# An attention block's scores in runs of three pairs, the row maxima turned in the scores' banks, and a changed start

## The reference

```python
def attn(x, Wq, bq, Wk, bk, Wv, bv, Wo, bo):      # x: (4, 512, 256), 16 heads of 16
    Q, K, V = (...)                                # x @ W.T + b, split into heads
    scores = jnp.einsum('bhqd,bhkd->bhqk', Q, K) / jnp.sqrt(jnp.float32(Hd))
    attn = jax.nn.softmax(scores, axis=-1)
    out = jnp.einsum('bhqk,bhkd->bhqd', attn, V)
    return out.transpose(0, 2, 1, 3).reshape(B, S, D) @ Wo.T + bo
x = x + attn(layernorm(x), ...)
x = x + ffn(layernorm(x), W1, W2, W3)              # silu(x W1') * (x W3'), Hadamard transform, W2
x = x + memory(layernorm(x), ...)
x = x + ffn(layernorm(x), W1, W2, W3)
```

## Time and profile before

| what | value |
|---|---|
| median of three runs | 586.15 us |
| the profiled execution | 586.26 us, of which the span from first to last instruction is 584.4 |
| TensorE busy | 565.8 us, 97% |
| VectorE busy | 376.8 us, 64% |
| ScalarE busy | 298.5 us, 51% |
| GpSimd busy | 176.6 us, 30% |
| granted TensorE clock | 0.999 |
| DMA | 26.54 MB, mean 45 GB/s |
| chain that ended last | TensorE 85%, VectorE 5%, ScalarE 4% |

### The profile page before, as it was taken

One profiled execution on the slowest core, in us unless ns is written; L12 is line 12 of the kernel. 1 busy time (PEld: TensorE's weight loads), 2 busy tenths in 40 slices (PEclk: granted clock), 3 DMA queues, 4 the chain that ended last, 5 costly groups with the idle time before them and its releaser, 6 DMA issues.

```text
span 584.4 us, 8867 instructions
## 1 busy us (share of the span) xinstructions
PE 565.8 (97%) x3288; PEld 390.1 (67%) x3288; DVE 376.8 (64%) x718; ACT 298.5 (51%) x546; POOL 176.6 (30%) x193
## 2 busy tenths in 40 slices
PE   9899999999999988999999999999999999999997
PEld 4534334344334433368888888898777888888886
DVE  5498898898888899644363444558887436344433
ACT  3238878876886787752334242244445233424221
POOL 3956446354455242820101010014333010101000
PEclk9999999999999999999999999999999999999999
DMA  7654740240033030010000000000000010010101
GB/s 231 135 112 163 199 122 18 76 127 20 2 111 109 3 146 3 3 72 2 1 0 1 1 0 1 2 2 0 1 0 2 1 36 1 1 36 2 38 0 37
DMA packets 17891, 26.54 MB, mean 45 GB/s; under 512 B 2552, under 2 KB 10744, under 8 KB 17464
## 3 DMA queue, kind: packets, MB, share of 16 engines
q1 hardware_dynamic: 15992, 24.13, 13.6%
q10 hardware_dynamic: 1856, 1.84, 1.4%
HBM read 10.88 MB, written 5.24 MB: 28 GB/s over the span
## 4 chain that ended last, share of the span: by engine, by line
PE 85%; DVE 5%; ACT 4%; issue 2%; DMA 1%; POOL 1%; SPq 1%; DVEq 0%; ACTq 0%
PE PS L281 82%; PE PS L292 2%; DVE mxr L861 2%; ACT PR L735 1%; DMA ring<-ql 1%; DVE PR L1020 1%; ACT xf L644 1%; ACT qf L658 1%; DVE XNs L842 1%; ACT PR L788 1%; POOL xTl L1051 1%; ACT xTh L644 1%; PE PS L472 1%; DVE AOl L853 1%; SPq L214 1%
## 5 line engine op out<-in xcount | busy, mean ns | idle before, releaser
L281 PE MATMUL PS<-xTh,ring 128*128 128x512 f32 x608 | 188.5, 392 | 0.0
L861 DVE TENSOR_REDUCE mxr<-PS 128x1 f32<-128x512 f32 x256 | 163.0, 682 | 29.0 <-PE PS L281 28.7
L735 ACT ACTIVATE PR<-PS 128x512 f32<-128x512 f32 x256 | 137.8, 603 | 39.7 <-PE PS L281 39.7
L281 PEld LDWEIGHTS PS<-xTh,ring 128*128 128x128 f32 x608 | 113.2, 188 | 22.9 <-issue 0.8
L281 PE MATMUL PS<-xTl,ring 128*128 128x512 f32 x304 | 110.3, 391 | 0.4 <-POOL xTl L1051 0.4
L281 PE MATMUL PS<-ring 50*128 50x512 f32 (+1 forms) x512 | 98.2, 450 | 5.4 <-DVE mxr L861 4.9
L975 DVE TENSOR_TENSOR PR<-PR,PS 128x512 f32<-128x512 f32 x64 | 43.8, 684 | 91.6 <-PE PS L281 73.7
L281 PEld LDWEIGHTS PS<-ring 50*128 50x128 f32 (+1 forms) x512 | 41.2, 184 | 84.2 <-ACT PR L735 57.2
L644 ACT ACTIVATE AOh<-PR 128x512 fp32r<-128x512 f32 x72 | 45.5, 632 | 101.1 <-DVE PR L975 89.2
L1051 POOL TENSOR_TENSOR xTl<-xf,xTh 128x512 fp32r<-128x512 f32 x30 | 43.2, 1456 | 140.9 <-ACT xTh L644 140.9
L853 DVE TENSOR_TENSOR AOl<-PR,AOh 128x512 fp32r<-128x512 f32 x72 | 51.1, 710 | 50.3 <-ACT AOh L644 50.3
(11 more groups left out here) (98 smaller groups left out, 621.5 us busy)
## 6 DMA issues: line engine op xcount, KB each, us to landing
ring<-qh SPq DMA_DIRECT2D x52, 128.0 KB, 3.1
ring<-ql SPq DMA_DIRECT2D x26, 128.0 KB, 3.1
ring<-weight_scratch SPq DMA_DIRECT2D x3, 1024.0 KB, 4.9
weight_scratch<-in_w SPq DMA_DIRECT2D x2, 1024.0 KB, 6.8
out<-X SPq DMA_DIRECT2D x8, 256.0 KB, 2.2
X<-in_x SPq DMA_DIRECT2D x3, 512.0 KB, 5.2
PR<-in_w SPq DMA_DIRECT2D x1, 1024.0 KB, 7.6
ring<-AOh SPq DMA_DIRECT2D x8, 128.0 KB, 4.0
```

The lines of the kernel that those rows point to most:

```text
L281: return nc.tensor.matmul(dst, lhsT, rhs, start=start, stop=stop, skip_group_check=True)
L735: nc.scalar.activation(PR[:, j % 8, :], PS[:, kq_bank(j), :], ACT.Exp, scale=HD ** -0.5)\
L861: nc.vector.tensor_reduce(mxr[:, S % 2, blk, TT * p + t:TT * p + t + 1], PS[:, QK0 + i % 3, :], AX.X, ALU.max, negate=True).then_inc(max_d ...
```

## The change

It has four parts.

1. *Runs of three pairs.* The loop now goes over the pairs j instead of the steps. The other work of step k comes in the gap behind pair `gap_of(k)`, the first j of the form 3i + 2 that isn't before 2k. So three pairs stand in a row, and the work of one or two steps behind them. Of every four gaps (six steps) two hold a piece from `shared_bank` and a value product, one only the value product, one only the piece.
2. *The turned maxima in the QK banks.* The turns of S = 1 to 14 no longer use `MB`: the list `slots` deals the three QK banks to QK scores and turns in the order in which TensorE makes them, and each waits for what had the bank three slots before (`wait_slot`). Nothing in `MB` waits for a turn any more, and a turn waits for nothing in `MB`. The turn of S = 15 stays in `MB`.
3. *The first rows of the ring.* The six transfers of a tile now alternate between the ring's halves. For tile 1 the four high parts go out from ScalarE's queue, beginning with the other half, and the two low parts from SyncE's queue behind its own six. The identity matrix is loaded ahead of the query weight.
4. *The rest of the start.* Four fillers instead of seven ahead of the transposes, one instead of three ahead of the scores, none in the second part of the lead; the Hadamard products four steps later; the second sequence normalised by ScalarE in two passes (with the negative means, `nmean`) instead of GpSimd; `wo` brought in by SyncE's queue and split in steps 3 and 5 of the loop.

```diff
-TAIL_BANKS = (2, 4, 5, 3, 0, 1)
+TAIL_BANKS = (2, 3, 4, 5, 0, 1)
+RUN = 3
-HAD_AT = (4, 5, 6, 8)
+HAD_AT = (8, 9, 10, 12)
...
+        def gap_of(K):
+
+            return (2 * K + 2 - (RUN - 1)) // RUN * RUN + RUN - 1 if RUN > 1 else 2 * K
+
+
+        turn_gap = {S: gap_of(8 * (S - 1) + MAX_AT) for S in range(1, LAST_GROUP - 1)}
+        slots = [("score", i) for i in range(2 * LEAD)]
+        for pair in range(TAIL):
+            slots.append(("score", pair + 2 * LEAD))
+            slots += [("turn", S) for S, gap in turn_gap.items() if gap == pair]
+        slot_of = {what: n for n, what in enumerate(slots)}
+
+        def qk_bank(i):
+            return QK0 + slot_of["score", i] % 3
...
-                    for blk in range(2) for r in rows(qk, part, blk)]
+                    for r in zip(*(rows(qk, part, blk) for blk in range(2))) for blk, r in enumerate(r)]
...
+            sp.wait_ge(qk_lo, 2)
+            for args in ring_rows(0, 1, 1):
+                sp.dma_start(*args).then_inc(ring_in[1], DMA)
...
+            def wait_slot(n):
+
+                if n >= 3:
+                    kind, i = slots[n - 3]
+                    pe.wait_ge(max_done if kind == "score" else mt_ready, i + 1)
+
+            def turn_max(S):
+                pe.wait_ge(ml_done, S + 1)
+                pe.wait_ge(mt_ready, S)
+                if S in turn_gap:
+                    wait_slot(slot_of["turn", S])
...
-                if 2 * U + h >= 3:
-                    pe.wait_ge(max_done, 2 * U + h - 2)
+                wait_slot(slot_of["score", 2 * U + h])
...
-            keep_busy(7, MB, SEQ)
+            keep_busy(4, MB, SEQ)
...
             pe.wait_ge(ring_in[0], QDMAS)
-            keep_busy(3, PS[:, 5, :], SEQ)
+            keep_busy(1, PS[:, 5, :], SEQ)
...
-            for K in range(STEPS * BATCH):
-                b, s = K // STEPS, K % STEPS
-                for h in range(2):
...
+            for j in range(2 * STEPS * BATCH):
+                K, h = j // 2, j % 2
+                wait_kq(K, h)
+                if K + LEAD < STEPS * BATCH:
+                    wait_qk(K + LEAD, h)
+                score_kq(K, h)
+                if K + LEAD < STEPS * BATCH:
+                    score_qk(K + LEAD, h)
+
+                for k in range(max(K - 2, 0), K + 1):
+                    if gap_of(k) == j:
+                        shared_bank(k, k // STEPS, k % STEPS)
+                        S = (k + LEAD) // 8 - 1
+                        if k % 8 == MAX_AT and S < LAST_GROUP:
+                            turn_max(S)
+                        if k % 2 and k >= 3:
+                            weigh_values((k - 3) // 2)
...
                 if n == 1:
-                    for part, ready in ((0, qk_hi), (1, qk_lo)):
-                        act.wait_ge(ready, 2)
-                        for args in ring_rows(0, 1, part):
-                            act.dma_start(*args).then_inc(ring_in[1], DMA)
+                    act.wait_ge(qk_hi, 2)
+                    for i in (1, 0, 3, 2):
+                        act.dma_start(*ring_rows(0, 1, 0)[i]).then_inc(ring_in[1], DMA)
```

More of the change, by code:

```diff
@@ L114, in kq_bank, with turn_bank @@
             return KQ0 + j % 3 if j < TAIL else TAIL_BANKS[(j - TAIL) % 6]
+        def gap_of(K):
[8 more added lines that the diff above has]
+            return QK0 + slot_of["score", i] % 3
+        def turn_bank(S):
+            return PS[:, QK0 + slot_of["turn", S] % 3, :] if S in turn_gap else MB
         wscr = nc.dram_tensor("weight_scratch", [3, P, KD * HID], F32, kind="Internal").ap()
@@ L130, in build @@
         first_in = [sem(f"first_in{t}") for t in range(TT)]
-        first_xns, wq_in, wk_in = (sem(n) for n in ("first_xns", "wq_in", "wk_in"))
+        first_xns, wq_in, wk_in, centred = (sem(n) for n in ("first_xns", "wq_in", "wk_in", "centred"))
+        nmean_done = sem("nmean_done")
         wv_in, wo_in, bias_in, ident_in, const_in, w2_in, ones_in = (
@@ L239, in _ @@
             max_rows(0)
+            for e in range(2):
+                for j in range(GH):
+                    r = 32 * j + HD * e
+                    sp.dma_start(OT[r:r + HD, :, :].rearrange("p a c -> p (a c)").rearrange("p (g n) -> p g n", n=D),
+                                 wo.rearrange("(g e) (j c) n -> e j c g n", e=2, c=32)[e, j, 0:HD, :, :])\
+                        .then_inc(wo_in, DMA)
             for b in range(BATCH):
@@ L348, in score_kq @@
                    ring[r:r + MROW + 2, b % 2, QI, p, :], True, True).then_inc(st_ready, 1)
+            def wait_slot(n):
[7 more added lines that the diff above has]
+                    wait_slot(slot_of["turn", S])
+                else:
+                    pe.wait_ge(x_done, 2 * BATCH - 3)
+                nc.tensor.transpose(turn_bank(S)[0:32, 0:P], ms[:, :, :, :].rearrange("p a b k -> p (a b k)"),
+                                    ident[:, :]).then_inc(mps_ready, 1)
             def wait_qk(U, h):
@@ L374, in weigh_values @@
                 pe.wait_ge(exp_done, 4 * a + 4)
+                if a == 0:
+                    pe.wait_ge(w2h_done, FT // 2)
                 if kt == 0:
@@ L441, in _ @@
                         .then_inc(mps_ready, 1)
-            pe.wait_ge(w2h_done, FT // 2)
+                if U == LEAD - 2:
+                    pe.wait_ge(xns_ready, 1)
+                    pe.wait_ge(mt_ready, 1)
+                    ln_transpose(0, MB)
             def shared_bank(K, b, s):
-                more, turned = b < BATCH - 1, K + LEAD
+                more = b < BATCH - 1
                 if s == LN_AT[0] and more:
                     pe.wait_ge(xns_ready, b + 2)
-                    pe.wait_ge(mt_ready, turned // 8)
+                    pe.wait_ge(v_copied, 2 * (b + 2))
                     ln_transpose(0, MB)
@@ L489, in shared_bank @@
                     else:
-                        pe.wait_ge(mt_ready, turned // 8)
+                        pe.wait_ge(x_f, 2 * (b + 1))
                     for part in range(2):
@@ L493, in shared_bank @@
                 if s in OUT_AT[1] and b:
-                    if s == OUT_AT[1][0]:
-                        pe.wait_ge(mt_ready, turned // 8)
+                    if s == OUT_AT[1][0] and more:
+                        pe.wait_ge(v_copied, 2 * (b + 1) + 1)
+                    elif s == OUT_AT[1][0]:
+                        pe.wait_ge(mt_ready, LAST_GROUP)
                     out_projection(1, OUT_AT[1].index(s))
@@ L507, in shared_bank @@
                     elif s == V_AT[1][0]:
-                        pe.wait_ge(mt_ready, turned // 8)
+                        pe.wait_ge(v_copied, 3)
                     project_v(b + 1, 1, V_AT[1].index(s))
-            for K in range(STEPS * BATCH):
-                b, s = K // STEPS, K % STEPS
-                for h in range(2):
-                    wait_kq(K, h)
-                    if K + LEAD < STEPS * BATCH:
-                        wait_qk(K + LEAD, h)
-                    score_kq(K, h)
-                    if K + LEAD < STEPS * BATCH:
-                        score_qk(K + LEAD, h)
-                shared_bank(K, b, s)
-                if K % 2 and K >= 3:
-                    weigh_values((K - 3) // 2)
+            for j in range(2 * STEPS * BATCH):
[14 more added lines that the diff above has]
+                            weigh_values((k - 3) // 2)
+            for k in range(STEPS * BATCH - 2, STEPS * BATCH):
+                if gap_of(k) >= 2 * STEPS * BATCH and k % 2:
+                    weigh_values((k - 3) // 2)
             weigh_values(STEPS * BATCH // 2 - 1)
@@ L754, in _ @@
                     ln_hi(b + 1, 1, 0)
+                if K == 3:
+                    act.wait_ge(wo_in, 8 * DMA)
+                    hi(WOh[:, :, :].rearrange("p g n -> p (g n)"), OT[:, :, :].rearrange("p a c -> p (a c)"))\
+                        .then_inc(whi_done, 1)
                 if s == 5 and b:
@@ L1122, in _ @@
             pool.wait_ge(vone_done, 1)
+            split_max(0)
             for g in range(GROUPS):
                 place_values(0, g)
-            pool.wait_ge(rstd_done, 2)
-            pool.wait_ge(lnT_ready, 2)
-            for t in range(TT):
-                last = normalise_tile(TT + t, TT + t, t)
-            last.then_inc(xns_ready, 1)
-            split_max(0)
-            pool.wait_ge(whi_done, 4)
-            lo(WOl[:, :, :].rearrange("p g n -> p (g n)"), OT[:, :, :].rearrange("p a c -> p (a c)"),
-               WOh[:, :, :].rearrange("p g n -> p (g n)")).then_inc(wol_done, 1)
             pool.wait_ge(zero_done, 1)
```

81 lines of the change are left out of this document (32 added, 49 removed).

## The result

The changed kernel takes 606.77 us (median of 4 executions, 603.56 to 624.57), the kernel before 586.25: ratio 1.0335, 95% interval [1.0309, 1.0361]. It is slower by some 19.6 us; 583.8 was predicted. The execution of 624.57 us, at a granted clock of 0.950 where the others had 0.980 to 0.991, is left out of the ratio. The profiled execution took 603.56 us (span 601.8).

The account below looks back on a forecast made before the run. TensorE's own order was taken to pace the first three attention stretches, VectorE's row maxima the fourth. Terms -4.5 - 7.7 - 1.2 + 5.0 + 6.5 + 0 - 0.5 = -2.4 us gave 583.8 us, range 576 to 590.5.

Parts of the forecast that it names:

- Start, -4.5: Before the loop: scores begin 4.0 us earlier, ring transfers give 0.3 and the first exponential 0.2; bounds -3.2 and -5.5.
- rival (4): At the start: transfers, not issue, set when ring rows land, near 25; 1.5 us gained, 586.8 us overall; chance 0.10.
- Fewer stops, -7.7: First three stretches: 32 fewer stops of 0.18 us, plus half the possible saving where fillings share a stop; bounds -5.8, -9.6.
- half term: Where two fillings share one stop, a return to the scores falls away: at most 0.12 x 32 = 3.8 us, half taken.
- No bank to spare, +5.0: Runs of three fill all three banks, so VectorE's maxima and other work delay short gaps; bounds 0 and 8.
- The turned maximum in the ring, +6.5: Turn takes a maximum bank, so TensorE waits for ScalarE's copy and its transfer; 8.0 us worked out, bounds 3 and 8.
- The five turns named: Turns S = 2, 5, 8, 11, 14: waits of 0.82 us for the copy and 0.78 for the transfer each.
- Shared bank, -1.2: Turned maxima no longer wait for the projections' bank, six waits of 1.2 us in all.
- Fourth stretch and tail, -0.5: Fourth stretch unchanged at 0, bounds -1.4 and +1; four stops of 0.18 us fewer in the last 13 steps.
- Rival (2): In the loop, both kinds of bank waits cost more than stops save: 588.3 us, or 590.2; chance 0.30.

Follow-up runs that it names:

- e12: Changed kernel with runs of two, maxima turned in the shared bank, four fillers instead of two before the ring's first rows: 584.20 us, ratio 0.9977.
- e5: Changed kernel with runs of two pairs and four fillers instead of two before the wait for the ring's first rows: 582.49 us, ratio 0.9941.
- e6: Changed kernel with ScalarE's copy of turned maxima ahead of the second exponential at S = 2, 5, 8, 11, 14, and four fillers instead of two: 595.06 us.
- e9: Changed kernel with four fillers instead of two before the wait for the ring's first rows: 602.34 us, ratio 1.0282.
- e1: Changed kernel with runs of two pairs and maxima turned in the shared bank, so only the new start remains: 587.12 us, ratio 1.0011.
- e2: Changed kernel with runs of two pairs instead of three, maxima still turned in the QK banks: 585.46 us, ratio 1.0015.
- e13: e6 with both row maxima and exponentials over 256 of 512 columns, part of the computation left out: 573.05 us, ratio 0.9779.
- e7: e6 with row maxima over 256 of 512 columns, part of the computation left out: 583.58 us, ratio 0.9956.
- e8: e6 with exponentials over 256 of 512 columns, part of the computation left out: 591.76 us, ratio 1.0083.
- e3: Changed kernel with maxima turned in the shared bank again, runs of three kept: 605.51 us, ratio 1.0334.
- e4: Changed kernel with ScalarE's copy of turned maxima moved ahead of the step's second exponential at S = 2, 5, 8, 11, 14: 602.19 us, ratio 1.0251.
- e10: e5 without the alternation of ring halves in the transfers, queues kept: 582.68 us, ratio 0.9943.

## Why the prediction was wrong

The runs form a chain from the kernel before to the changed one: start -1.3 (e12), turned maxima in the ring -2.1 (e5 against e12), runs of three +12.7 (e6 against e5: 0.0217 x 586), the late copy +7.3 (e9 against e6), two fillers fewer +3.1 (the changed kernel against e9). Such a chain gives the measured 19.6 us whatever the causes are, so the sum proves nothing; what each part rests on is the one edit between its two kernels. The clock lies in several of them. A mean clock short of 1 by some share costs at most that share of the time: by the mean clocks of the executions in the ratios at most 0.4 us in e5, 1.3 in e6, 4.3 in e9 and 8.6 in the changed kernel. So by this estimate at least 11 of the 19.6 us would be there at full clock. By the steps of the prediction:

- **Start, -4.5: the step that failed is that fewer fillers only save time.** The issue into the ring moved by the 2.3 us worked out, but the rows took 1.2 us longer to land, so that the scores begin 2.8 us earlier; rival (4) named this and gave it 1.5 us. In e12 the loop's second transposes come at 42.66 against 45.45, and the feed-forward at 249.76 against 252.00: 0.5 is given back in the first stretch, where it wasn't looked for further. And the fillers that were taken away had covered part of a stand: 1.65 us became 2.88, and 0.63 with four fillers in e9. The prediction gave a fall of the clock during waits no chance of its own, because a wait of 1.65 us had left it at 1.00; it cost 2.0 us in e1 and 4.3 in e2. In the changed kernel the same two fillers are worth about 3, but no trace shows that this is the start: its profiled execution has no fall there. The falls make single executions of the same kernel differ by 10 us.
- **Fewer stops, -7.7: right in kind, too large by the half term, and hidden.** A run of two and one of three take 0.67 and 0.90 without waits, which leaves 0.21 for the stop; 0.18 was taken. There were 92 runs in the three stretches and not 96, so 28 stops fell away and not 32: 5.9 us, where the working had 5.8. For the fillings that come directly behind each other nothing shows up: value product and projection take 46.8 and 31.4 us with shared stops, 46.8 and 31.8 without. That half term (1.9 us) was wrong. The 5.9 us appear only in e13, and there by 2.3.
- **No bank to spare, +5.0 of up to 8: the main failure.** Measured are 20.6 - 4.3 = 16.3 us in the three stretches (e6 against e5). The working had 10 in it (7 for VectorE's other work in short gaps, 32 x 0.05 to 0.1 of the bare limit) and halved them by sums paid before and by catching up. Two errors. The catching up isn't there: VectorE's busy time is no reserve when the third maximum of a run has to be done before the third pair of the next, and other work in a short gap comes back in the run behind it: with 0.42 of statistics in the gap the run at 125.42 takes 1.45 us in place of 0.91. And a wait wasn't priced: the turn needs the bank of the first pair of its own run, 3.9 us in eight waits in the changed kernel and 4.2 in e6, where the copy comes early.
- **The turned maximum in the ring, +6.5, bounds 3 to 8: right in size at full clock.** The five turns named wait 0.68 for the copy and 0.43 to 1.45 for the transfer, 7.0 us in all, four of them in the three stretches, and moving the copy gives 7.3 us back, falls of the clock included. The 0.4 us of waiting for the copy at S = 1, 4, 7, 10 isn't there; all of those turns, and S = 3, 6 and 9, have the turn's own wait instead.
- **Shared bank, -1.2: right, too small.** The turn in the ring is worth -2.1 with runs of two (e12, e5).
- **Fourth stretch and tail, -0.5: wrong.** +6.3 us in the profiled execution. Of these 51.90 - 49.03 = 2.9 are the clock, by e9's window at 1.00; the other 49.03 - 45.57 = 3.5 are there at full clock, where VectorE is at the limit (stands of 0.84 and 0.44 us for its maxima at 234 and 237 us) and the late copy of S = 14 costs 0.68 and 1.45. In e7, with half the maxima and the early copy, that part takes 45.84 as in e5 with runs of two.

Rival (2), that the two bank waits cost more than the stops save, is what happened, with a price of 588 to 590 us. Its price ended where the bounds ended (8 + 8), while the waits for banks alone came to 16.3 us, and the clock was outside of all of them. What stays open is why the clock falls in the loop of one execution and not of another, since no kernel was run in which TensorE is kept busy through those waits.

## What to carry to other kernels

Before an engine's work is drawn together into longer runs, count the buffers against the run: where a run is as long as the ring, the last buffer of the former run has to be free before this one ends, other work on the engine that frees them stands in the open, and idle time elsewhere on it doesn't pay it back. Half the work on the suspected engine (e7, e8) shows in one run who holds them, which the list of waits doesn't, since waits inside a pipelined run count as busy. Don't take filler matmuls away by their own time alone: look how long the engine will stand where they stood, and at the granted clock of several executions, since one profile may miss the fall.

## What the hardware did that was not expected

- Waits of the same length go with a fall of the clock in one execution and with none in another. Executions of one kernel show it too: e6's have mean clocks of 1.000, 1.000, 0.997 and 0.994. TensorE stood 2.88 us in the changed kernel's profiled execution, 1.52 in e12's and 2.17 in e3's without a fall; it fell with 3.01 us in e2, 2.65 in e1 and 2.57 in e4, and even with four fillers behind 1.66 us, in the profiled execution of e13, whose other four executions took 572.2 to 574.1 against its 582.5:

```profile
24.02 1.13 PE L315 MATMUL PS<-AOf 128*128 128x512 f32 x2 [1.66 <-DMA ring<-ql]
```

```profile
24.00:28.00 4.00, 3.98 (x9) 0.66 0.25 82
28.00:32.00 4.00, 4.00 (x10) 0.50 0.61 206
32.00:40.00 8.00, 8.00 (x15) 0.50 0.16 55
```

- Once down it stayed down for 3 us (e1), 7 (e2) or some 20 (e4, e13), though TensorE had the same sequence of scores and fillers before it in all four and counted as busy throughout.
- Inside the loop, waits of 0.68 and 0.69 us with 1.8 us of work between them were followed by a fall (152 to 156 us). The Trainium skill (TensorE: Matmul & The Clock Gate, A second HAM failure mode: psum-queue depth-cycling) describes this: an engine that stands briefly again and again between groups of matmuls, while it goes round its banks, has its clock lowered and raised again, and its throughput falls by that. This case's traces agree in part: in the changed kernel 1.4 us of waits at 152 to 155 us, and 0.50 of the clock from 156 to 158. But three other pairs of such waits in the same trace, and all five in e9's, were followed by none. That the waits make the clock fall is not shown.
- Transfers into the ring that were issued 2.3 us earlier took 1.2 us longer to land; alternating between the halves of the partitions changed that by nothing that can be measured (e10), and the queues weren't tried apart.
